# The gram's spread form with the sequence as the innermost index: one core, 32 images, windowed and axial attention

## The chip, the cores and the metric

The kernel runs on one core of one Trainium2 chip. The metric is the device time of one execution in microseconds (us), the median of several runs.

## What is computed

Two residual blocks on x of shape (32, 16, 16, 256). The first is shifted-window attention with cosine logits, a position bias, a mask and a softmax. The second, which the change is in, is axial attention without a softmax, once along the rows and once along the columns of each image. Both start with a group norm. Cut to what matters:

```python
def _self_attention(x, w_qkv, w_out, heads):          # x: sequences of 16 tokens, 256 channels
    q, k, v = jnp.split(x @ w_qkv, 3, axis=-1)         # 16 heads of 16
    dots = jnp.einsum('bhie,bhje->bhij', q, k) * d ** (-0.5)
    out = jnp.einsum('bhij,bhje->bhie', dots, v)
    return out.transpose(0, 2, 1, 3).reshape(b, t, d) @ w_out

x = x + window_attention(_gn(x), ...)                  # layer 0
h = _gn(x)                                             # layer 1
x = x + _self_attention(columns of h, w_qkv0, w_out0) + _self_attention(rows of h, w_qkv1, w_out1)
```

Since there is no softmax in the axial layer, (q kT) v is computed as q (kT v). The 16 x 16 matrix kT v of a head and a sequence is the "gram" of this kernel.

## The kernel before

Channels lie on the 128 partitions in two groups (G = 2), tokens in the free dimension. Every f16 operand of a matmul is kept as a high and a low part (value = high + low), and products are made in passes high*high, low*high, high*low. The kernel works on the images in a software pipeline written out by hand: each engine has a `step(k)` that issues, for several images at different stages, its instructions in a fixed order, with semaphore waits (`reach`) between engines. One step is one image's worth of work on every engine. The index a is 0 for the column pass and 1 for the row pass of the axial layer; everything below is done once for each a and image.

The stages that touch the gram, in order:

- `gram_matmuls` (L598 to L611, TensorE) makes kT v of 32 sequences (2 groups of 16) and 16 heads, into two PSUM banks, one for each parity of head in a pair.
- `gram_high` (L894, ScalarE) takes the two banks one after the other, scales each by a per-partition mask (a head's 16 partitions of 32) and writes the f16 high part: two ACTIVATE of 128 x 512. `gram_low` (L1347, VectorE) writes the low part, bank value times mask minus high part: two SCALAR_TENSOR_TENSOR of 128 x 512, which read the high part from SBUF. Both go through `gram_half` (L330), which says where in SBUF they write.
- `spread_gram` (L422, the queue of SyncE) copies the gram into `gram_wide`, four DMAs of 32 partitions each: `gram_wide` has four slots q of 32 columns, and partitions 32q to 32q + 31 are copied into slot q alone; the rest stays zero from a memset at the start. So each sequence has in `gram_wide` a block-diagonal 128 x 128 matrix, high and low.
- `axial_out` (L613, TensorE) multiplies: for each of 32 sequences the high matrix is loaded as the stationary operand and meets q's high and low part (32 columns, L620), then the low matrix is loaded and meets q's high part (16 columns, L621). That is 64 weight loads of 128 x 128 and 64 short matmuls for each a and image, 4,096 over the kernel.

In a step of TensorE the order is: gram_matmuls(0), axial_kv(0), window_out, a wait for `gram_lo[0]` (the low part by VectorE, as the PSUM banks are used again), gram_matmuls(1), window_v, image_channels, axial_kv(1), result_rows, axial_out(0), axial_y, scores, axial_q(1), axial_q(0), axial_out(1), window_den, window_pv, window_qk. axial_out(a) waits for `gram_spread[a]`, that is, for the landing of the four DMAs.

The per-partition layout before is, from the outermost index to the innermost: sequence s (32), [slot q (4) in gram_wide], column e (32), part t (2: high, low), of 2 bytes each.

Of the kernel before, what the change touches and what calls it, by code (L numbers as in the profile page):

```python
# [11 lines left out]
F32 = mybir.dt.float32  # L12
F16 = mybir.dt.float16

P = 128
IMAGES, SIDE, D = 32, 16, 256
TOK = SIDE * SIDE
G = D // P
HEADS, DH = 16, 16
# [4 lines left out]
SEQ = SIDE  # L24
# [36 lines left out]
def reach(eng, sem, img, per=1, j=None):  # L61

    if not missing(img.n):
        eng.wait_ge(sem, img.n * per + (per if j is None else j))


def is_first(img):
    return img.n == 0
# [39 lines left out]
def build(nc, x, Wq, Wk, Wv, bv, Wo, bo, logit_scale, cpb_w1, cpb_b1, cpb_w2, w_qkv0, w_out0, w_qkv1, w_out1,  # L108
          c_ident, c_group, c_small, c_mask, c_coords, out, scratch):
    ctx = ExitStack()  # L110
    with ctx:
        def sb(name, shape, dt=F32):
            return ctx.enter_context(nc.sbuf_tensor(name, shape, dt))

        def sem(name):
            return ctx.enter_context(nc.semaphore(name))
# [46 lines left out]
        kv32 = [sb(f"kv32_{a}", [P, 2, HALF]) for a in range(2)]  # L163
        kv = [sb(f"kv_{a}", [P, 2, 2, 2 * D], F16) for a in range(2)]
        v_wide = [sb(f"v_wide{a}", [P, 4, 2, 2, D], F16) for a in range(2)]
        gram_both = sb("gram", [P, 2, G * SEQ, 32, 2], F16)
        gram = [gram_both[:, a] for a in range(2)]
        gram_wide = [sb(f"gram_wide{a}", [P, G * SEQ, 4, 32, 2], F16) for a in range(2)]
        o1_32 = [sb(f"o1_32_{a}", [P, HALF]) for a in range(2)]
        o1 = [sb(f"o1_{a}", [P, 2, HALF], F16) for a in range(2)]  # L170
        y = sb("y", [P, HALF])
# [30 lines left out]
        wide_zeroed = sem("wide_zeroed")  # L202
# [50 lines left out]
        gram_spread = [sem(f"gram_spread{a}") for a in range(2)]  # L253
# [75 lines left out]

        def gram_half(a, head, t):  # L330

            return gram[a][:, :, DH * head:DH * head + DH, t]

        def gram_psum(a, head, img):

# [2 lines left out]
        def gram_place(g, s):  # L338

            return 16 * (s // 4 % 2) + 8 * g + 4 * (s // 8) + s % 4  # L340
# [29 lines left out]
        def _(sp):  # L370
# [51 lines left out]
            def spread_gram(a, img):  # L422

                if is_first(img):
                    sp.wait_ge(wide_zeroed, ZEROED)
                reach(sp, gram_lo[a], img)
                for q in range(4):
                    rows = slice(32 * q, 32 * q + 32)
                    sp.dma_start(gram_wide[a][rows, :, q].rearrange("p s e t -> p s (e t)"),  # L429
                                 gram[a][rows].rearrange("p s e t -> p s (e t)")).then_inc(gram_spread[a], 16)  # L430

            def spread_v_rows(a, img):

# [13 lines left out]
            def step(k):  # L447
                for img in there(k - 6):
                    spread_v_rows(0, img)
                    spread_v_rows(1, img)  # L450
                for img in there(k - 10):
                    store_image(img)
                for img in there(k - 6):
                    spread_gram(0, img)
                for img in there(k):
                    load_image(img)
                for img in there(k - 6):
                    spread_gram(1, img)
# [9 lines left out]
            spread_v_rows(1, pic[0])  # L468
            load_image(pic[4])
            spread_gram(0, pic[0])  # L470
            load_image(pic[6])
            spread_gram(1, pic[0])
# [9 lines left out]
        def _(pe):  # L482
# [130 lines left out]
            def axial_out(a, img):  # L613
                reach(pe, gram_spread[a], img, 64)
                for s in range(G * SEQ):
                    cols = slice(s * SEQ, (s + 1) * SEQ)
                    dst = ps[:, O_BANK[a](img) + s // SEQ, (s % SEQ) * 2 * SEQ:(s % SEQ + 1) * 2 * SEQ]
                    at = gram_place(*divmod(s, SEQ))
                    high, low = (gram_wide[a][:, at, :, :, gp].rearrange("p h e -> p (h e)") for gp in range(2))
                    pe.matmul(dst.rearrange("p (t i) -> p t i", t=2), high, q1[a][:, :, cols], start=True, stop=False)  # L620
                    last = pe.matmul(dst[:, 0:SEQ], low, q1[a][:, 0, cols], start=False, stop=True)  # L621
                last.then_inc(o1_done[a], 1)
# [38 lines left out]
            def step(k):  # L661
# [23 lines left out]
                for img in there(k - 4):  # L685
                    reach(pe, xt_copied, earlier(img, -4))
                    edge(pe, qk_scaled, earlier(img, -3))
                    axial_out(0, img)
# [18 lines left out]
                for img in there(k - 4):  # L707
                    reach(pe, biased[1], earlier(img, -3))
                    axial_out(1, img)
# [70 lines left out]
            pe.wait_ge(qk_scaled, 4)  # L780
            pe.wait_ge(xt_copied, 5)
            axial_out(0, pic[0])
            pe.wait_ge(gram_lo[1], 1)
            group_means(0, pic[4])
# [50 lines left out]
        def _(act):  # L835
# [58 lines left out]
            def gram_high(a, img):  # L894

                reach(act, gram_done[a], img)
                reach(act, gram_spread[a], previous(img), 64)
                for head in range(2):
                    last = act.activation(gram_half(a, head, 0), gram_psum(a, head, img), ACT.Copy,  # L899
                                          scale=gram_mask[:, head:head + 1])  # L900
                last.then_inc(gram_hi[a], 1)
# [227 lines left out]
        def _(pool):  # L1129

            pool.memset(v_diag[:].rearrange("p a b c d -> p (a b c d)"), 0.0).then_inc(zeroed, 1)
            pool.memset(gram_wide[0][:].rearrange("p s q e t -> p (s q e t)").bitcast(F32), 0.0).then_inc(wide_zeroed, 1)
            pool.wait_ge(first_in, 16 * 3)

            def zero_v_wide():
# [98 lines left out]

        @block.vector
        def _(dve):
            dve.memset(gram_wide[1][:].rearrange("p s q e t -> p (s q e t)").bitcast(F32), 0.0).then_inc(wide_zeroed, 1)
            dve.wait_ge(first_in, 16 * 3)

            def cap_scale():  # L1240
# [106 lines left out]
            def gram_low(a, img):  # L1347

                reach(dve, gram_hi[a], img)
                reach(dve, o1_done[a], previous(img))  # L1350
                for head in range(2):
                    last = dve.scalar_tensor_tensor(gram_half(a, head, 1), gram_psum(a, head, img), gram_mask[:, head:head + 1],  # L1352
                                                    gram_half(a, head, 0), ALU.mult, ALU.subtract)
                last.then_inc(gram_lo[a], 1)
# [274 lines left out]
```

## Time and profile before

| | |
|---|---|
| median of 3 runs | 912.56 us (911.0 to 913.3) |
| the profiled execution | 910.2 us, of which the span of instructions 908.4 us |
| TensorE busy | 846.0 us, 93% |
| VectorE busy | 730.3 us, 80% |
| ScalarE busy | 666.0 us, 73% |
| GpSimd busy | 493.0 us, 54% |
| mean granted TensorE clock | 0.972 of full speed |
| DMA, the queue of SyncE | 331,728 packets, 71.10 MB, 37.8% of 16 engines |

The profile is of one execution, whose own time is 1.8 us over its span. A share of busy time is a mean over start, steady steps and end. TensorE's matmuls are pipelined, so their single durations overlap; what a group of matmuls costs is read from the start of its first to the start of what follows.

### The profile page before, as it was taken

How to read it: one execution, taken by the hardware profiler on the slowest of the kernel's cores; microseconds unless marked ns; L12 is line 12 of the kernel's file. 1: busy time of each engine (PE TensorE's matmuls, PEld its weight loads, DVE VectorE, ACT ScalarE, POOL GpSimd, SP SyncE). 2: the span in 40 equal slices, each digit the busy share in tenths (PEclk: the TensorE clock that was granted, in tenths of full speed). 3: DMA queues.
4: the chain of work that ended last, by engine and by line, in shares of the span. 5: the costliest groups of instructions: out<-in, count | busy, mean ns of one | idle time of the engine just before them, and what ended most of it. 6: DMA issues, size and time to landing. Idle time of an engine off the chain costs nothing.

```text
span 908.4 us, 45985 instructions
## 1 busy us (share of the span) xinstructions
PE 846.0 (93%) x20128; PEld 660.0 (73%) x20128; DVE 730.3 (80%) x1528; ACT 666.0 (73%) x1112; POOL 493.0 (54%) x366
## 2 busy tenths in 40 slices
PE   5478899999999999999999999999999999999865
PEld 3354677777878877777877777778787777777554
DVE  7879888888888988888888888888889888886431
ACT  3666677887777787887777878877778778777441
POOL 4545455565565565565565565655655655655321
PEclk9698999999999999999999999999999999999888
DMA  6201344434334444434334444343444443343433
GB/s 165 57 13 40 74 80 80 78 77 88 78 82 82 92 91 90 84 80 90 79 78 87 86 92 91 74 88 78 85 81 91 90 92 70 72 81 78 92 74 82
DMA packets 334431, 74.04 MB, mean 82 GB/s; under 512 B 282373, under 2 KB 333719, under 8 KB 334231
## 3 DMA queue, kind: packets, MB, share of 16 engines
q1 hardware_dynamic: 331728, 71.10, 37.8%
q8 instruction: 158, 2.59, 1.3%
q10 hardware_dynamic: 2502, 0.01, 0.2%
q14 instruction: 43, 0.34, 0.1%
HBM read 12.31 MB, written 8.40 MB: 23 GB/s over the span
## 4 chain that ended last, share of the span: by engine, by line
PE 76%; SPq 7%; DVE 6%; issue 4%; DMA 3%; ACT 3%; POOL 1%; POOLq 0%; DVEq 0%; ACTq 0%
PE ps L518 20%; PE ps L588 15%; PE ps L631 9%; PE ps L620 7%; PE ps L609 6%; PE ps L535 4%; SPq L439 4%; PE ps L621 4%; PE ps L550 3%; PE ps L559 3%; PE ps L568 3%; SPq L429 2%; DMA gram_wide<-gram 2%; PE ps L658 2%; PE ps L652 1%
## 5 line engine op out<-in xcount | busy, mean ns | idle before, releaser
L1147 POOL TENSOR_TENSOR kv<-kv,kv 128x1024 f16<-128x1024 f32 x64 | 137.0, 2141 | 90.0 <-ACT kv L882 84.6
L930 ACT ACTIVATE probs<-probs 128x1024 f32<-128x1024 f32 x64 | 67.8, 1059 | 91.9 <-DVE probs L1407 89.7
L620 PEld LDWEIGHTS ps<-q,gram_wide 128*128 128x128 f16 x2048 | 107.5, 97 | 13.2 <-DMA gram_wide<-gram 5.4
L620 PE MATMUL ps<-q,gram_wide 128*128 128x32 f16 x2048 | 111.6, 177 | 5.4 <-DMA gram_wide<-gram 5.3
L1152 POOL TENSOR_TENSOR stat<-stat,small 128x2 f32<-128x2 f32 x64 | 43.3, 693 | 133.1 <-DVE stat L1326 125.3
L1352 DVE SCALAR_TENSOR_TENSOR gram<-ps,small,gram 128x512 f16<-128x512 f32 x128 | 94.5, 793 | 23.0 <-ACT gram L899 19.8
L621 PE MATMUL ps<-q,gram_wide 128*128 128x16 f16 x2048 | 110.7, 169 | 0.0
L621 PEld LDWEIGHTS ps<-q,gram_wide 128*128 128x128 f16 x2048 | 106.2, 97 | 0.4
L518 PE MATMUL ps<-xn,w_q 128*128 128x256 f16 x768 | 97.4, 278 | 7.0 <-POOL xn L1147 7.0
L899 ACT ACTIVATE gram<-ps,small 128x512 f16<-128x512 f32 x128 | 95.3, 817 | 8.0 <-PE ps L609 8.0
L1147 POOL TENSOR_TENSOR xn<-xn,xn 128x512 f16<-128x512 f32 x64 | 74.9, 1170 | 47.7 <-ACT xn L919 47.7
L631 PE MATMUL ps<-o,w_o 128*128 128x256 f16 x768 | 91.2, 276 | 3.0 <-POOL o L1147 2.8
L588 PE MATMUL ps<-w_kv,xn 128*128 128x512 f16 x384 | 90.7, 387 | 2.8 <-ACT kv L882 1.9
L588 PE MATMUL ps<-w_kv,xn_cols 128*128 128x512 f16 x384 | 90.5, 386 | 0.5 <-POOL xn_cols L1147 0.3
L1147 POOL TENSOR_TENSOR qk<-qk 128x1024 f16<-128x1024 f32 x32 | 69.0, 2157 | 38.7 <-ACT qk L950 38.7
L1147 POOL TENSOR_TENSOR o<-o,o 128x512 f16<-128x512 f32 x64 | 74.3, 1162 | 26.1 <-ACT o L913 25.8
L518 PEld LDWEIGHTS ps<-xn,w_q 128*128 128x128 f16 x768 | 71.3, 99 | 20.1 <-POOL xn L1147 5.4
L1407 DVE TENSOR_TENSOR probs<-ps,bias_mask 128x1024 f32<-128x1024 f32 x64 | 75.5, 1219 | 12.6 <-PE ps L550 12.6
L631 PEld LDWEIGHTS ps<-o,w_o 128*128 128x128 f16 x768 | 76.0, 102 | 12.6 <-POOL o L1147 3.0
L609 PE MATMUL ps<-v_wide,kv 64*32 64x128 f16 x6144 | 69.1, 225 | 11.7 <-DVE o L1358 5.6
L1147 POOL TENSOR_TENSOR xn_cols<-xn,xn_cols 128x512 f16<-128x512 f32 x32 | 45.3, 1416 | 62.4 <-ACT xn_cols L925 62.4
L1365 DVE STREAM_TRANSPOSE qk<-qk_sq 128x1024 f32<-128x1024 f32 x32 | 39.9, 1245 | 47.7 <-ACT qk_sq L935 47.7
(122 smaller groups left out, 1961.2 us busy)
## 6 DMA issues: line engine op xcount, KB each, us to landing
gram_wide<-gram SPq DMA_DIRECT2D x256, 128.0 KB, 3.1
v_wide<-kv SPq DMA_DIRECT2D x512, 32.0 KB, 2.3
x_in<-x SPq DMA_DIRECT2D x32, 128.0 KB, 2.4
x_in<-x SPq DMA_DIRECT2D x64, 64.0 KB, 2.3
out<-y_out SPq DMA_DIRECT2D x32, 128.0 KB, 2.2
out<-y_out SPq DMA_DIRECT2D x64, 64.0 KB, 2.0
x<-L_conv_w_qkv SPq DMA_DIRECT2D x1, 768.0 KB, 4.4
y_out<-L_conv_w_out SPq DMA_DIRECT2D x2, 256.0 KB, 4.8
```

Of the source, the lines that this page charges most:

```text
L518: last = pe.matmul(dst, w[:, wp, c, m * P:m * P + P], act[:, xp, c * TOK:(c + 1) * TOK], start=(n == 0), stop=(n == 5))
L588: last = pe.matmul(ps[:, KV_BANK[a](img) + t, :], xn1[a][:, xp, c * TOK + t * P:c * TOK + t * P + P], w_l1[a]["kv"][:, wp, c, :], start=(n ...
L609: last = pe.matmul(dst.rearrange("p (s e) -> p s e", e=32), kv[a][rows, kp, t, own], v_wide[a][rows, :, vp, t, own], start=(n == 0), stop= ...
L620: pe.matmul(dst.rearrange("p (t i) -> p t i", t=2), high, q1[a][:, :, cols], start=True, stop=False)
L621: last = pe.matmul(dst[:, 0:SEQ], low, q1[a][:, 0, cols], start=False, stop=True)
L631: last = pe.matmul(ps[:, Y_BANK(img), g * TOK:(g + 1) * TOK], w_l1[a]["o"][:, wp, c2, g * P:(g + 1) * P], o1[a][:, xp, c2 * TOK:(c2 + 1) * ...
L899: last = act.activation(gram_half(a, head, 0), gram_psum(a, head, img), ACT.Copy, scale=gram_mask[:, head:head + 1])
L930: act.activation(part, part, ACT.Exp).then_inc(probs_ready[g], 1)
L1147: return pool.tensor_tensor(dst, whole, high, ALU.subtract)
L1152: pool.tensor_tensor(stat[layer][:, 28:30], stat[layer][:, 26:28], minus_half, ALU.pow).then_inc(gn_pow[layer], 1)
L1352: last = dve.scalar_tensor_tensor(gram_half(a, head, 1), gram_psum(a, head, img), gram_mask[:, head:head + 1], gram_half(a, head, 0), ALU. ...
L1407: dve.tensor_tensor(probs[:, 4 * g:4 * g + 4, :].rearrange("p a n -> p (a n)"), ps[:, S_BANK[g](img):S_BANK[g](img) + 2, :].rearrange("p b ...
```

## The change

The per-partition layout of the gram and of its spread form is turned: slot q (in gram_wide), column e, sequence s, part t. So the elements of one sequence's matrix, which are the columns of a weight load, lie 128 bytes apart in place of 4 bytes; ScalarE's and VectorE's writes, and VectorE's read of the high part, walk the columns of a sequence in the same order as before and so step by 128 bytes in place of 4 too; and what one partition sends in one DMA of the spread is one run of 4,096 bytes in source and destination, in place of 32 runs of 128 bytes. The two memsets cover the same bytes. The arithmetic and its order are the same.

```diff
-        gram_both = sb("gram", [P, 2, G * SEQ, 32, 2], F16)
+        gram_both = sb("gram", [P, 2, 32, G * SEQ, 2], F16)
         gram = [gram_both[:, a] for a in range(2)]
-        gram_wide = [sb(f"gram_wide{a}", [P, G * SEQ, 4, 32, 2], F16) for a in range(2)]
+        gram_wide = [sb(f"gram_wide{a}", [P, 4, 32, G * SEQ, 2], F16) for a in range(2)]
@@ gram_half
-            return gram[a][:, :, DH * head:DH * head + DH, t]
+            return gram[a][:, DH * head:DH * head + DH, :, t].rearrange("p e s -> p s e")
@@ spread_gram
-                    sp.dma_start(gram_wide[a][rows, :, q].rearrange("p s e t -> p s (e t)"),
-                                 gram[a][rows].rearrange("p s e t -> p s (e t)")).then_inc(gram_spread[a], 16)
+                    sp.dma_start(gram_wide[a][rows, q].rearrange("p e s t -> p (e s t)"),
+                                 gram[a][rows].rearrange("p e s t -> p (e s t)")).then_inc(gram_spread[a], 16)
@@ axial_out
-                    high, low = (gram_wide[a][:, at, :, :, gp].rearrange("p h e -> p (h e)") for gp in range(2))
+                    high, low = (gram_wide[a][:, :, :, at, gp].rearrange("p h e -> p (h e)") for gp in range(2))
```

No instruction is added, removed or moved on TensorE, VectorE, ScalarE or GpSimd. On the queue of SyncE every instruction keeps its place as well; only the shape of the spread's DMAs differs. A step there before (v_wide is the spread of v, x_in a coming image, out a finished one):

```order
L439 DMA v_wide<-kv 16x4x256 x16
L429 DMA gram_wide<-gram 32x32x64 x4
L420 DMA x_in<-x 128x256
L420 DMA x_in<-x 64x256 x2
L429 DMA gram_wide<-gram 32x32x64 x4
```

and the same rows of the change:

```order
L439 DMA v_wide<-kv 16x4x256 x16
L429 DMA gram_wide<-gram 32x2048 x4
L420 DMA x_in<-x 128x256
L420 DMA x_in<-x 64x256 x2
L429 DMA gram_wide<-gram 32x2048 x4
```

Nothing moved; each of the four DMAs of a spread goes from 32 x 32 pieces of 64 elements to 32 pieces of 2,048.

## Rows read from the trace of the kernel before

**Rows 1.** The page: busy time of the engines; granted clock in 40 slices.

```profile
PE 846.0 (93%) x20128; PEld 660.0 (73%) x20128; DVE 730.3 (80%) x1528; ACT 666.0 (73%) x1112; POOL 493.0 (54%) x366
PEclk9698999999999999999999999999999999999888
```

**Rows 2.** Busy time by stretch (us from the span's start): steady state, one step, two axial_out.

```profile
core 0: us, PE busy (x) PEld busy (x) DVE busy (x) ACT busy (x) POOL busy (x), PEclk, DMA share, GB/s
200.00:800.00 600.00, 598.30 (x14647) 473.32 (x14646) 512.72 (x1105) 472.72 (x791) 344.34 (x256) 1.00 0.41 84
395.49:421.09 25.60, 25.60 (x637) 20.16 (x644) 22.08 (x47) 20.37 (x35) 14.92 (x12) 1.00 0.42 87
406.20:408.00 1.80, 1.80 (x67) 1.74 (x65) 1.80 (x4) 1.69 (x2) 1.80 (x1) 1.00 0.28 73
888.40:890.20 1.80, 1.80 (x65) 1.80 (x66) 0.00 (x0) 0.00 (x0) 0.00 (x0) 0.50 1.09 180
```

**Rows 3.** Timeline of TensorE, axial_out(0) of a steady step: start us, us, instruction.

```profile
406.27 0.18 PE L620 MATMUL ps<-q,gram_wide 128*128 128x32 f16 x1
406.30 0.17 PE L621 MATMUL ps<-q,gram_wide 128*128 128x16 f16 x1
...
407.86 0.17 PE L621 MATMUL ps<-q,gram_wide 128*128 128x16 f16 x1
```

**Rows 4.** The same view, the last axial_out of the kernel.

```profile
888.39 0.21 PE L620 MATMUL ps<-q,gram_wide 128*128 128x32 f16 x1 [3.90 <-DMA gram_wide<-gram]
...
890.10 0.17 PE L621 MATMUL ps<-q,gram_wide 128*128 128x16 f16 x1
```

**Rows 5.** The same view, gram_matmuls(1) of a steady step and what follows it.

```profile
400.47 1.00 PE L609 MATMUL ps<-v_wide,kv 64*32 64x128 f16 x96
401.40 0.39 PE L535 MATMUL ps<-w_v,xn 128*128 128x256 f16 x2
```

**Rows 6.** By source line: duration ns min/median/max, first and last start us, forms.

```profile
L919 ACT ACTIVATE xn<-xn x64: 612/630/642, 13.3 to 853.1; 128x512 f16<-128x512 f32 x64
L875 ACT ACTIVATE w_o<-y_out x2: 612/614/617, 32.6 to 46.2; 128x512 f16<-128x512 f32 x2
L875 ACT ACTIVATE w_kv<-x x1: 1045/1045/1045, 30.7 to 30.7; 128x1024 f16<-128x1024 f32 x1
L925 ACT ACTIVATE xn_cols<-xn x32: 1050/1084/1092, 58.4 to 853.6; 128x512 f16<-128x512 f32 x32
L899 ACT ACTIVATE gram<-ps,small x128: 777/819/837, 85.3 to 884.2; 128x512 f16<-128x512 f32 x128
L1352 DVE SCALAR_TENSOR_TENSOR gram<-ps,small,gram x128: 748/788/833, 87.4 to 885.7; 128x512 f16<-128x512 f32 x128
```

**Rows 7.** Timeline of ScalarE and VectorE between gram_matmuls(0) and gram_matmuls(1) of that step.

```profile
395.42 1.12 PE L609 MATMUL ps<-v_wide,kv 64*32 64x128 f16 x96
396.03 1.01 ACT L935 ACTIVATE qk_sq<-ps 128x1024 f32<-128x1024 f32 x1
396.94 1.49 ACT L899 ACTIVATE gram<-ps,small 128x512 f16<-128x512 f32 x2
398.46 1.46 DVE L1352 SCALAR_TENSOR_TENSOR gram<-ps,small,gram 128x512 f16<-128x512 f32 x2
```

**Rows 8.** Waits: who waited for whom, us in total, times, longest.

```profile
PE ps L620 <- DMA gram_wide<-gram: 5.3, 4, 3.9
```

**Rows 9.** By source line, the DMA issues of SyncE's queue: ns each.

```profile
L429 SPq DMA_DIRECT2D gram_wide<-gram x256: 585/675/2154, 88.9 to 888.6; - x128
L439 SPq DMA_DIRECT2D v_wide<-kv x512: 585/596/1828, 71.7 to 879.8; - x171
```

**Rows 10.** The page: DMA issues, KB each, median us from issue to landing.

```profile
gram_wide<-gram SPq DMA_DIRECT2D x256, 128.0 KB, 3.1
x_in<-x SPq DMA_DIRECT2D x32, 128.0 KB, 2.4
out<-y_out SPq DMA_DIRECT2D x32, 128.0 KB, 2.2
```

**Rows 11.** Groups by line and form: weight loads, busy us, mean ns | idle before.

```profile
L658 PEld LDWEIGHTS ps<-stat,group 128*128 128x128 f32 x128 | 19.4, 192 | 10.2 <-DVE stat L1312 3.4 <-ACT v_diag L964 2.2 <-issue 2.1
L620 PEld LDWEIGHTS ps<-q,gram_wide 128*128 128x128 f16 x2048 | 107.5, 97 | 13.2 <-DMA gram_wide<-gram 5.4 <-DVE probs L1407 5.3 <-issue 1.8
```

More of the change, by code:

```diff
@@ L1131, in _ @@
             pool.memset(v_diag[:].rearrange("p a b c d -> p (a b c d)"), 0.0).then_inc(zeroed, 1)
-            pool.memset(gram_wide[0][:].rearrange("p s q e t -> p (s q e t)").bitcast(F32), 0.0).then_inc(wide_zeroed, 1)
+            pool.memset(gram_wide[0][:].rearrange("p q e s t -> p (q e s t)").bitcast(F32), 0.0).then_inc(wide_zeroed, 1)
             pool.wait_ge(first_in, 16 * 3)
@@ L1236, in _ @@
         def _(dve):
-            dve.memset(gram_wide[1][:].rearrange("p s q e t -> p (s q e t)").bitcast(F32), 0.0).then_inc(wide_zeroed, 1)
+            dve.memset(gram_wide[1][:].rearrange("p q e s t -> p (q e s t)").bitcast(F32), 0.0).then_inc(wide_zeroed, 1)
             dve.wait_ge(first_in, 16 * 3)
```

## The prediction

> **What bounds the kernel now.** I read the page first: TensorE is busy 93% of the span, VectorE 80%, ScalarE 73%, GpSimd 54% [rows 1]. That is a mean over start, middle and end, so next the stretches: between 200 and 800 us TensorE is busy 598.3 of 600 us at full granted clock, and one step is 25.60 us with all of it TensorE, 22.08 VectorE, 20.37 ScalarE [rows 2]. Twenty-odd of the 32 steps look like this. In steady state TensorE is the bound and waits for nobody; what the change does to TensorE's own work arrives in full, and what it does to others arrives only past their slack.
>
> Then the stage that reads the changed buffer. axial_out issues 64 weight loads and 64 short matmuls. Its first matmul starts at 406.27 and its 64th at 407.86 [rows 3]: 1.59 us over 63 intervals is 25.2 ns for a load and its matmul. The matmuls themselves move 32 or 16 columns; at 2.4 GHz (granted clock 1.00 in that stretch, [rows 2]) that is 13 and 7 ns, so they don't set the pace. What does? Two rows speak for the weight load's read of SBUF. In the last axial_out, after a wait of 3.90 us, the granted clock is 0.50, that is 1.2 GHz [rows 2], and the pace is (890.10 - 888.39)/63 = 27.1 ns [rows 4]: half the clock, nearly the same pace, so it isn't counted in TensorE's cycles. And 96 loads with matmuls of gram_matmuls take 401.40 - 400.47 = 0.93 us, 9.7 ns each [rows 5], so the issue of instructions isn't it either. What is left is something of fixed time in loading 128 columns of f16, about 0.2 ns a column.
>
> **The change, part by part.** Nothing is added or moved; four things cost differently.
>
> (1) The weight loads, 4,096 in all. Their columns lie 128 bytes apart in place of 4. No TensorE read in the trace steps that far, so the price has to be bounded. Below: nothing, if the load doesn't care. The nearest row that shows what a wide step costs is ScalarE's. L919 and L925 are the same copy of 512 elements from f32 to f16; L925 reads them 64 bytes apart. They take 630 and 1,084 ns, 454 ns more [rows 6]. A copy of 1,024 elements takes 1,045 and one of 512 614, so an element costs 431/512 = 0.84 ns, and the wide step adds 454/512 = 0.89 ns: it costs each element about once more [rows 6]. If a weight load whose pace is a read of SBUF doubles likewise, 25.2 becomes 50.4 ns: 64 x 2 x 25.2 ns = 3.23 us a step, x 32 = 103.2 us. Above: if the load loses whatever makes it quick, the f32 load of 128 columns shows what a slow one looks like, 192 ns beside 97 [rows 11], 95 ns more, 389 us in all. I take the doubling, since it is the same memory and the same kind of step.
>
> The Trainium skill's page "SBUF — State Buffer" (under "Door 1", the note on cachelines) says that SBUF has 16-byte lines and that at least two accesses must fall in a line for full speed. A step of 4 bytes has four f16 in a line, one of 128 bytes has one. ScalarE's pair of rows agrees; no row shows it for TensorE. By that rule the load is slowed, the sum of this step is of the kind taken above, and the rule speaks against this change.
>
> (2) ScalarE's and VectorE's halves of the gram, 128 instructions each, two and two for each a. They write with a step of 128 bytes in place of 4, and VectorE also reads the high part so. Per stream and instruction: at least nothing (the rows show no wide write), at most L925's 0.454 us. A step of theirs that matters is a = 0: gram_matmuls(0) starts at 395.42, ScalarE squares first (396.03 for 1.01), then its two (396.94 for 1.49), VectorE's two (398.46 for 1.46, so to 399.92), and gram_matmuls(1), which waits for them, starts at 400.47 [rows 5, 7]. Slack 0.55 us. Queued behind ScalarE's pair are the high part of o1 and the copies of kv; behind VectorE's the sum over heads, whose users come later; behind the wait on TensorE all of the step. With (1) slower, TensorE comes to this place 1.6 us later in each step and the square is no longer late: its pair can start some 0.35 us sooner after gram_matmuls(0), slack 0.9 us. The six streams (two instructions on ScalarE with one, two on VectorE with two) cost 0 to 2.72 us; I take half, 1.36, as nothing shows a write: 0.46 us late, x 32 = 15 us. Both ends: 0 and (2.72 - 0.9) x 32 = 58 us. For a = 1 there is more room: axial_out(1) comes near the end of the step.
>
> (3) The spread's DMAs: 32 pieces of 4,096 bytes each in place of 1,024 of 128. Landing takes 3.1 us; loads and stores of the same 128 KB in longer runs take 2.4 and 2.2 [rows 10]. Issue takes 675 ns, for v_wide 596 [rows 9]. So up to 0.9 us + 4 x 0.08 = 1.2 us a spread, but TensorE waited for a spread four times in the whole kernel, 5.3 us, 3.9 of it once, at the end [rows 8]. In steady state this transfer is hidden behind TensorE's other work, and halving it buys nothing. I take 3 us (0 to 5).
>
> [...] TensorE's steady step has no wait in it and its matmuls go at the pace of their columns, so I book 0.
>
> Sum against the profiled execution's own 910.2 us (span 908.4): + 103.2 + 15 - 3 = 1,025.4. The median of the runs shown is 912.56, 2.4 above it: 1,027.8, so 1,028.
>
> **The rivals.**
>
> *The load doesn't care, and the writers do.* The 25.2 ns may be a floor under any full-array pair, with the load's own time well below it, so that even a doubled load stays hidden. Against it stands that the pace hardly moved with the clock, which a floor of fixed time would explain too. Then only (2) is left, with slack 0.55: (1.36 - 0.55) x 32 = 26 us, less 3: 936 us; bounds 912 and 979. VectorE would also come close to being the bound itself: 22.08 + 4 x 0.91 = 25.7 of 25.6 us a step.
>
> The Trainium skill's "TensorE: Matmul & The Clock Gate", "Back-to-back issue gap", gives matmuls of 1 to 64 columns a floor of about 60 cycles, some 25 ns, and its section on fast weight load names packed or strided columns as its read pattern, with steps far over 64 elements allowed. By these rules the load could be free in this change. The trace agrees on 25 ns at 2.4 GHz; at 1.2 GHz it shows 27.1 [rows 4], where 60 cycles would be 50.
>
> *Nothing shows.* Neither load nor writers care, or their surcharge stays in the slack, and the DMA's gain is a microsecond or two: 911 us.
>
> *The other side: faster.* All of that, and the spread lands about a microsecond sooner wherever the chain passes through it. It is decided by the fill and the drain: three or four spreads of the first and last images at 1.2 us each, bounded by the 5.3 us of waits [rows 8]. 912.6 - 4 = 908.6 us. It needs the surcharge on the load to be under about 0.3 ns (1.2 us over 4,096), and the writers' under the slack.
>
> *The load falls to the slow form.* 25.2 becomes some 120 ns, + 389 us: 1,300 us. Nothing in the trace speaks for it but that a step so wide is new.
>
> **How the numbers follow.** Chances: doubled load 0.50; load unchanged with late writers 0.15; nothing shows 0.11; faster 0.18; slow form 0.06. What can be told from no change is about 0.3%, 2.7 us. Slower is the first, the second and the last: 0.71; same 0.11; faster 0.18. The doubled load's own range is 990 (a surcharge of three quarters of the load) to 1,071 (912.6 + 103 + 58 - 3). The range for all must reach down to the cases that leave the load alone: 908 to 1,071, which leaves out the slow form, half of the faster case and the fringe of the first, some 0.17.
>
> **What the profile after would show.** Step 1: the pace of axial_out, first start to 64th, near 3.2 us in place of 1.59; the step 25.6 to about 29 us; VectorE's and ScalarE's share falling as the span grows. If the pace is unchanged, step 1 is wrong, and with it the forecast. Step 2: L899 and L1352 above 819 and 788 ns, and a wait of TensorE at gram_matmuls for VectorE's gram; if their means stand, the 15 us are wrong. Step 3: some 8,000 packets in place of 262,144 for the spread, DMA share far below 37.8%, landing under 3.1 us, and no gain from it in the middle of the kernel. The wait before the last axial_out under 3.9 us.

## The result, and the profile after

The changed kernel takes 1,500.26 us (median of 4 runs, 1,499.76 to 1,502.17) against 912.93 us of the kernel before: a ratio of 1.644, 95% interval 1.639 to 1.648. The forecast's direction was right and its size was far off: 587 us more, where 115 were forecast and 158 were the top of the range.

The page of the changed kernel, to be held against [rows 1] and the packets in the table of before:

```profile
PE 1243.7 (83%) x20128; PEld 996.5 (66%) x20128; DVE 992.1 (66%) x1528; ACT 879.9 (59%) x1112; POOL 498.0 (33%) x366
...
PEclk8886878788887878787878788878888787878766
...
q1 hardware_dynamic: 77776, 71.10, 19.6%
...
gram_wide<-gram SPq DMA_DIRECT2D x256, 128.0 KB, 2.7
```

Every engine but GpSimd is busy for longer, TensorE no longer all the time, and the granted clock, which was full through the whole middle [rows 1, 2], lies at 0.7 or 0.8 in 37 of 40 slices. The DMAs did what was asked: a quarter of the packets, half the share, landing in 2.7 in place of 3.1 us [rows 10].

Then the lines that the change touches, by source line (duration ns min/median/max), to be held against [rows 6]:

```profile
L620 PEld LDWEIGHTS ps<-q,gram_wide x2048: 162/217/254, 107.8 to 1485.2; 128*128 128x128 f16 x187
...
L899 ACT ACTIVATE gram<-ps,small x128: 2534/2682/2828, 88.3 to 1466.7; 128x512 f16<-128x512 f32 x128
...
L1352 DVE SCALAR_TENSOR_TENSOR gram<-ps,small,gram x128: 2500/2690/2995, 93.2 to 1471.9; 128x512 f16<-128x512 f32 x128
```

ScalarE's and VectorE's instructions on the gram went from 819 and 788 ns to 2,682 and 2,690, both by 1.9 us. The same part of a steady step as in [rows 3, 5, 7] (timeline: start us, us, instruction, the idle time before it and its releaser):

```profile
713.20 1.00 PE L609 MATMUL ps<-v_wide,kv 64*32 64x128 f16 x96
...
714.25 4.85 ACT L899 ACTIVATE gram<-ps,small 128x512 f16<-128x512 f32 x2
716.73 1.47 PE L518 MATMUL ps<-o,w_o 128*128 128x256 f16 x12
719.13 4.78 DVE L1352 SCALAR_TENSOR_TENSOR gram<-ps,small,gram 128x512 f16<-128x512 f32 x2 [3.53 <-ACT gram L899]
723.97 1.48 PE L609 MATMUL ps<-v_wide,kv 64*32 64x128 f16 x96 [5.77 <-DVE gram L1352]
...
731.66 0.26 PE L620 MATMUL ps<-q,gram_wide 128*128 128x32 f16 x1 [0.50 <-ACT x_t L989]
...
734.46 0.23 PE L621 MATMUL ps<-q,gram_wide 128*128 128x16 f16 x1
...
737.27 0.23 PE L621 MATMUL ps<-q,gram_wide 128*128 128x16 f16 x1
```

Between 713.20 and 723.97 the reader sees the chain of [rows 7] stretched: ScalarE's pair 4.85 us in place of 1.49, VectorE's pair 4.78 in place of 1.46, and TensorE idle for 5.77 us before gram_matmuls(1). From 731.66 to 737.27 the 64 loads of axial_out go at 5.61/63 = 89 ns, where they went at 25.2. And busy time by stretch, to be held against [rows 2]: one step, its axial_out(0), and axial_y behind it.

```profile
core 0: us, PE busy (x) PEld busy (x) DVE busy (x) ACT busy (x) POOL busy (x), PEclk, DMA share, GB/s
713.20:757.60 44.40, 38.13 (x630) 30.82 (x629) 30.33 (x47) 27.00 (x34) 14.98 (x12) 0.81 0.20 49
731.66:737.36 5.70, 5.70 (x65) 5.70 (x65) 5.63 (x7) 2.76 (x3) 2.21 (x1) 0.70 0.02 4
737.80:741.80 4.00, 4.00 (x25) 3.02 (x26) 3.97 (x9) 2.33 (x6) 0.00 (x0) 0.63 0.18 40
```

A step is 44.40 us in place of 25.60. In axial_out TensorE is shown busy without a gap and its granted clock still falls; it comes out of it at 1.2 GHz and runs the next stage so.

From the starts of TensorE's stages in this step and in that of before, the 18.80 us come out in full:

| where in the step | before, us | after, us | more |
|---|---|---|---|
| axial_out(0) and (1), start to next start | 1.67 + 1.69 | 5.70 + 5.76 | 8.10 |
| window_out to gram_matmuls(1), the wait for the gram | 1.40 | 7.24 | 5.84 |
| result_rows to axial_out(0), a wait for ScalarE | 0.52 | 1.10 | 0.58 |
| axial_y (L631) | 2.62 | 4.06 | 1.44 |
| window_den and window_pv (L559, L568) | 1.98 | 3.22 | 1.24 |
| gram_matmuls(1) and window_v (L609, L535) | 2.26 | 3.56 | 1.30 |
| all else | 13.46 | 13.76 | 0.30 |

The last four rows, 4.3 us, are for the most part stages whose own work didn't change and that stand behind a slow axial_out or behind the wait, at the lower clock.

### The profile page after: what moved, and what is told of

Read it like the earlier page. It is cut to its first block, busy times and chain, and to the rows that moved or that the text cites. A ratio compares the mean times of both kernels' runs of the same rounds, so it can differ in the third digit from the quotient of the medians.

```text
span 1498.6 us, 45985 instructions
## 1 busy us (share of the span) xinstructions
PE 1243.7 (83%) x20128; PEld 996.5 (66%) x20128; DVE 992.1 (66%) x1528; ACT 879.9 (59%) x1112; POOL 498.0 (33%) x366
## 4 chain that ended last, share of the span: by engine, by line
PE 58%; issue 16%; ACT 15%; DVE 10%; DMA 0%; SPq 0%; POOL 0%; ACTq 0%; POOLq 0%; DVEq 0%
PE ps L620 13%; PE ps L518 12%; ACT gram L899 11%; PE ps L621 10%; PE ps L631 9%; DVE gram L1352 6%; PE ps L559 4%; PE ps L568 3%; PE ps L609 2%; PE ps L550 2%; DVE head_sum L1372 2%; PE ps L658 1%; PE ps L588 1%; ACT head_rnorm L942 1%; ACT x_t L988 1%
## 5 line engine op out<-in xcount | busy, mean ns | idle before, releaser
L1352 DVE SCALAR_TENSOR_TENSOR gram<-ps,small,gram 128x512 f16<-128x512 f32 x128 | 316.9, 2683 | 141.8 <-ACT gram L899 141.8
L620 PEld LDWEIGHTS ps<-q,gram_wide 128*128 128x128 f16 x2048 | 361.6, 216 | 32.9 <-ACT x_t L989 20.2
L620 PE MATMUL ps<-q,gram_wide 128*128 128x32 f16 x2048 | 367.2, 244 | 18.6 <-ACT x_t L989 13.5
L621 PE MATMUL ps<-q,gram_wide 128*128 128x16 f16 x2048 | 365.4, 233 | 0.0
L621 PEld LDWEIGHTS ps<-q,gram_wide 128*128 128x128 f16 x2048 | 363.4, 217 | 0.0
L899 ACT ACTIVATE gram<-ps,small 128x512 f16<-128x512 f32 x128 | 311.1, 2685 | 17.3 <-PE ps L609 17.0
L609 PE MATMUL ps<-v_wide,kv 64*32 64x128 f16 x6144 | 80.8, 268 | 186.4 <-DVE gram L1352 182.0
L609 PEld LDWEIGHTS ps<-v_wide,kv 64*32 64x32 f16 x6144 | 67.5, 105 | 202.4 <-DVE gram L1352 190.9
L631 PE MATMUL ps<-o,w_o 128*128 128x256 f16 x768 | 137.2, 361 | 2.4 <-POOL o L1147 2.4
L631 PEld LDWEIGHTS ps<-o,w_o 128*128 128x128 f16 x768 | 102.3, 136 | 34.7 <-POOL o L1147 2.8
L892 ACT ACTIVATE q<-ps 128x512 f16<-128x512 f32 x64 | 37.9, 592 | 113.4 <-PE ps L621 107.6
L907 ACT ACTIVATE o<-ps 128x512 f32<-128x512 f32 x64 | 38.1, 595 | 107.3 <-PE ps L621 107.3
```

The costliest lines, as they stand in the source:

```text
L609: last = pe.matmul(dst.rearrange("p (s e) -> p s e", e=32), kv[a][rows, kp, t, own], v_wide[a][rows, :, vp, t, own], start=(n == 0), stop= ...
L631: last = pe.matmul(ps[:, Y_BANK(img), g * TOK:(g + 1) * TOK], w_l1[a]["o"][:, wp, c2, g * P:(g + 1) * P], o1[a][:, xp, c2 * TOK:(c2 + 1) * ...
```

## The experiments

**Four theories at the start.** A: three prices add up, slow loads, slow writers, and a clock that falls behind the slow loads as well as behind the wait. B: the clock falls only where TensorE waits. C: loads and writers slow each other at the memory. D: VectorE's busy time alone is the bound. Where columns land permuted the values differ and the work does not. "One run" below means a time without an interval. The kernel before lay between 908.6 and 915.4 us in all of its runs beside these, and every such time is at least 239 us away from it, but for that of side_f32_wide (916.64), which can't be told from no change; there the duration of one instruction is what is read.

**loads_wide: only the loads are wide.**

```diff
 (the changed kernel, with the gram and the writers of before)
-        gram_both = sb("gram", [P, 2, 32, G * SEQ, 2], F16)
+        gram_both = sb("gram", [P, 2, G * SEQ, 32, 2], F16)
-            return gram[a][:, DH * head:DH * head + DH, :, t].rearrange("p e s -> p s e")
+            return gram[a][:, :, DH * head:DH * head + DH, t]
```

> Only the weight loads step by 128 bytes; ScalarE, VectorE and the gram buffer are as before, and the spread moves the same 4,096-byte runs (the gram's columns land permuted, so the values are not the reference's; no work is left out). Theory A (three prices that add up: slow loads, slow writers, and a clock that falls behind the slow loads as well as behind the wait): the pace of axial_out is 89 ns as in the changed kernel, 8.2 us more a step, and the clock still falls after each of the two axial_out, about 2.9 us more a step: 36.7 us a step, about 1,260 us; the writers stay at 0.82 and 0.79 us. Rival B (the clock falls only because TensorE waits for the gram): full clock, 33.8 us a step, about 1,175 us. Rival C (loads are slow because slow writers hold the memory): pace 25 ns, about 913 us.

Measured: 1,276.24 us, ratio 1.398 (1.390 to 1.406). One step of it, its axial_out(0), axial_y, window_den with window_pv, in the columns of [rows 2]:

```profile
724.94:762.46 37.52, 37.52 (x630) 30.68 (x629) 22.55 (x47) 20.68 (x34) 15.04 (x12) 0.82 0.25 59
735.73:741.30 5.57, 5.57 (x67) 5.57 (x65) 3.20 (x9) 1.75 (x2) 1.95 (x1) 0.84 0.45 101
741.30:746.50 5.20, 5.20 (x28) 3.83 (x28) 1.25 (x5) 2.59 (x6) 0.00 (x0) 0.52 0.18 43
755.95:759.50 3.55, 3.55 (x82) 2.48 (x80) 1.55 (x4) 2.56 (x4) 0.74 (x1) 0.50 0.36 100
```

TensorE has no idle time in the step, and the clock is at 0.52 and 0.50 behind both axial_out: B falls. The pace is 5.57 us for 64 loads with the writers fast, so C falls for the loads. Of 11.92 us more a step, 7.85 are the loads themselves and 4 the clock behind them. A held, 16 us over its number.

**turned_walk: the changed kernel, with the writers' loops the other way round.**

```diff
 (the changed kernel; [...] stands for the two banks)
-            return gram[a][:, DH * head:DH * head + DH, :, t].rearrange("p e s -> p s e")
+            return gram[a][:, DH * head:DH * head + DH, :, t]
-            return ps[...].rearrange("p b (x e) -> p (b x) e", e=32)[:, :, DH * head:DH * head + DH]
+            return ps[...].rearrange("p b (x e) -> p (b x) e", e=32)[:, :, DH * head:DH * head + DH].rearrange("p s e -> p e s")
```

> The changed kernel with ScalarE's and VectorE's walk turned: sequences innermost, so writes and the read of the high part step by 4 bytes again, and PSUM is read with a step of 128 bytes instead. Layout, spread and weight loads stay those of the change. Theory A (the writers pay for the step of consecutive writes to SBUF): L899 and L1352 fall to between 0.8 and 1.3 us, the wait for the gram is at most 1 us a step, and the time is that of loads_wide, about 1,260 us. Rival E (it is the layout as a whole, or any operand with a wide step, PSUM's too): they stay at 2.7 us, about 1,500 us.

Measured: 1,276.01 us, ratio 1.398 (1.389 to 1.406). The writers by source line:

```profile
L899 ACT ACTIVATE gram<-ps,small x128: 805/831/845, 86.3 to 1242.8; 128x512 f16<-128x512 f32 x128
...
L1352 DVE SCALAR_TENSOR_TENSOR gram<-ps,small,gram x128: 773/794/948, 88.4 to 1244.3; 128x512 f16<-128x512 f32 x128
```

The same layout, the same bytes; only the order in which an instruction writes them changed, and 2.68 and 2.69 us became 0.83 and 0.79, while PSUM is now read in steps of 128 bytes, which costs ScalarE 12 ns. E falls: the price is of the step between consecutive accesses to SBUF (high_wide, below, tells the write from the read). It gives back 224 us of the 587.

**writers_wide: only the writers are wide.**

```diff
 (the kernel before)
-        gram_both = sb("gram", [P, 2, G * SEQ, 32, 2], F16)
+        gram_both = sb("gram", [P, 2, 32, G * SEQ, 2], F16)
-            return gram[a][:, :, DH * head:DH * head + DH, t]
+            return gram[a][:, DH * head:DH * head + DH, :, t].rearrange("p e s -> p s e")
-                                 gram[a][rows].rearrange("p s e t -> p s (e t)")).then_inc(gram_spread[a], 16)
+                                 gram[a][rows].rearrange("p e s t -> p (e s t)").rearrange("p (x y) -> p x y", y=64)).then_inc(gram_spread[a], 16)
```

> Only ScalarE's and VectorE's halves of the gram step by 128 bytes; gram_wide, the weight loads with 4-byte steps and the 128-byte runs of the spread are as before (the columns land permuted; no work is left out). Theory A: the writers take 2.7 us each as in the changed kernel, TensorE waits some 6 us a step at gram_matmuls(1) and runs some 1.3 us a step at the low clock behind it: 33 us a step, about 1,150 us; pace of axial_out 25 ns. Rival C (loads and writers slow each other): the writers stay near 0.8 us and the time near 913 us. Rival D (VectorE's busy time alone is the bound, 22.1 + 4 x 1.9 = 29.7 us a step): about 1,045 us.

Measured: 1,363.26 us, ratio 1.493 (1.484 to 1.502). All of the numbers were too low; the writers take 2.69 and 2.61 us as A said (so C falls for the writers too), but the step is 39.3 us, not 33. A step by busy time:

```profile
616.03:655.33 39.30, 30.21 (x632) 22.40 (x630) 30.01 (x47) 26.86 (x35) 14.87 (x12) 0.87 0.27 54
```

The gram's pieces in the chain of waits of the next step (start us, us, what):

```profile
658.66 2.79 ACT gram L899
...
663.61 2.65 DVE gram L1352
...
668.52 2.81 ACT gram L899 x2
...
677.02 4.79 DVE gram L1352 x2
```

TensorE is busy 30.21 of 39.30 us and VectorE 30.01: no engine is the bound, a chain is. It goes round the step through both passes' pairs: gram_high(0), gram_low(0), the sum over heads that is queued behind it on VectorE, its square roots on ScalarE, gram_high(1) queued behind these, the image copy queued behind that, the image's statistics on VectorE, gram_low(1), and from there the mask of k, the biases and the softmax's sums to the next step. Each of the four pairs grew by some 3.35 us, 13.4 us in all; by the two spans a step is (1,362.4 - 908.4)/32 = 14.2 us longer. That 25.60 + 13.4 = 39.0 comes so near to the 39.3 of this step is in part luck: 25.60 was TensorE's work, and how long this chain was before was not measured. D falls too.

**rows_wide: the writers of one pass only.**

```diff
 (the kernel before)
+            if a == 1:
+                turned = gram[a].rearrange("p s e t -> p (s e) t").rearrange("p (e s) t -> p e s t", s=G * SEQ)
+                return turned[:, DH * head:DH * head + DH, :, t].rearrange("p e s -> p s e")
             return gram[a][:, :, DH * head:DH * head + DH, t]
```

> The kernel before with the writers of the row pass alone (a = 1) in steps of 128 bytes; the column pass, the spread and the loads as before (columns of one pass permuted; no work left out). The prediction held that a = 1 has room. Theory S (all four pairs of the gram lie one after the other in one chain round the step, 25.6 + 4 x 3.35 = 39.0 us for writers_wide): with two pairs slow 25.6 + 6.7 less a little slack, 31 to 32 us a step, 1,090 to 1,120 us. Theory of the prediction: 913 to 930 us.

Measured: 1,152.43 us, one run. A step of it:

```profile
562.63:596.57 33.94, 28.40 (x629) 21.66 (x628) 27.24 (x48) 23.57 (x34) 14.80 (x11) 0.90 0.31 63
```

33.9 us in this step, 8.3 more, and 7.6 by the two spans, (1,150.6 - 908.4)/32, where two slow pairs are 6.7: S is the right kind and was put too low. Where the rest comes from stays open. It is not shown to be the clock (mean 0.90): the granted clock is below full from 568.0 to 580.3 us alone (0.84, then 0.64), where the chain runs through ScalarE and VectorE, and 1.00 where it comes back to TensorE. The pass that the prediction gave room costs more than half of writers_wide's surcharge (239 of 449 us).

**high_wide: a wide write, and a wide read beside a narrow write.**

```diff
 (the kernel before)
+            if t == 0:
+                turned = gram[a].rearrange("p s e t -> p (s e) t").rearrange("p (e s) t -> p e s t", s=G * SEQ)
+                return turned[:, DH * head:DH * head + DH, :, 0].rearrange("p e s -> p s e")
             return gram[a][:, :, DH * head:DH * head + DH, t]
```

> The kernel before with the high part alone written in steps of 128 bytes by ScalarE; VectorE reads it so but writes the low part in steps of 4 bytes; spread and loads as before (columns permuted; no work left out). Theory A (it is the write that costs, a wide read about one element time more): L899 2.7 us, L1352 0.79 + 0.45 = 1.2 us, and TensorE's wait for the gram about half of that of writers_wide: 3.8 + 0.9 - 0.55 = 4.1 us a step, about 1,060 us. Rival F (a wide read costs as much as a wide write): L1352 2.7 us and the time of writers_wide, about 1,150 us.

Measured: 1,194.61 us, one run; its lines are shifted by three.

```profile
L902 ACT ACTIVATE gram<-ps,small x128: 2534/2682/2836, 86.2 to 1166.6; 128x512 f16<-128x512 f32 x128
...
L1355 DVE SCALAR_TENSOR_TENSOR gram<-ps,small,gram x128: 1076/1094/1158, 91.1 to 1170.5; 128x512 f16<-128x512 f32 x128
```

VectorE pays 306 ns for reading 512 elements in wide steps, 0.6 ns each, and ScalarE 1,863 ns for writing as many, 3.6 ns each. F falls. The whole was 135 us above A's number. The chain through both passes' pairs accounts for it: four writes at 1.863 us and four reads at 0.306 us more are 8.7 us a step, and by the two spans it is (1,192.8 - 908.4)/32 = 8.9.

**step8, step16, step32, step64: where does the price begin?** The layout with K sequences inside the column (K = 2, 4, 8, 16; 1 is the kernel before, 32 the change). VectorE's instruction is cut in 2, 4, 4 and 2 pieces, as it takes only two free dimensions.

```diff
 (the kernel before; KS = 2, 4, 8 or 16; the writers' and the spread's lines, turned to match, are left out)
-        gram_both = sb("gram", [P, 2, G * SEQ, 32, 2], F16)
+        gram_both = sb("gram", [P, 2, G * SEQ // KS, 32, KS, 2], F16)
-        gram_wide = [sb(f"gram_wide{a}", [P, G * SEQ, 4, 32, 2], F16) for a in range(2)]
+        gram_wide = [sb(f"gram_wide{a}", [P, G * SEQ // KS, 4, 32, KS, 2], F16) for a in range(2)]
-                    high, low = (gram_wide[a][:, at, :, :, gp].rearrange("p h e -> p (h e)") for gp in range(2))
+                    high, low = (gram_wide[a][:, at // KS, :, :, at % KS, gp].rearrange("p h e -> p (h e)") for gp in range(2))
```

> The layout halfway: two sequences inside the column, so a column's step is 8 bytes for writers and loads and a run of the spread 256 bytes; VectorE's instruction is cut in two (256 elements each) since it takes only two free dimensions. Everything is computed. Theory L (the price starts where fewer than two accesses fall in 16 bytes): nothing costs more, pace of axial_out 25 ns, L899 0.82 us; VectorE's extra starts cost 0.6 us a step inside its slack: 913 us within 0.5%. Theory G (the price grows with every doubling of the step): pace above 27 ns, 920 to 950 us.

> Four sequences inside the column: step 16 bytes, runs of 512 bytes, VectorE's instruction in four. Everything is computed. Theory L: every access is a new line from here on, so the loads are at the changed kernel's 89 ns and the writers at 2.7 us already: about 1,500 us. Theory G: loads 35 to 50 ns, L899 about 1.1 to 1.3 us: 1,000 to 1,100 us.

> Eight sequences inside the column: step 32 bytes, runs of 1,024 bytes, VectorE's instruction in four. Everything is computed. Theory L: as the changed kernel, pace 89 ns and L899 2.7 us, about 1,500 us. Theory G: loads 50 to 70 ns, L899 1.5 to 2 us, 1,150 to 1,300 us.

> Sixteen sequences inside the column: step 64 bytes, runs of 2,048 bytes, VectorE's instruction in two. Everything is computed. Theory L: pace 89 ns, L899 2.7 us, about 1,500 us. Theory G: loads 65 to 80 ns, L899 2 to 2.4 us, 1,300 to 1,400 us.

Measured, with the kernel before, the change and pad144 (below) beside them; the pace of a load is (start of the 64th - start of the first)/63 of an axial_out in the middle of the run (within a run they differ by up to 4.5 ns):

| step of a column | load, ns | ScalarE's write of 512 (median ns) | whole kernel, us |
|---|---|---|---|
| 4 bytes (before) | 25.2 | 819 | 913 |
| 8 (step8) | 33.2 | 1,406 | 1,058.8, ratio 1.162 (1.156 to 1.169) |
| 16 (step16) | 60 | 2,664 | 1,421.0, ratio 1.557 (1.549 to 1.565) |
| 32 (step32) | 62 | 2,550 | 1,405.6, one run |
| 64 (step64) | 62.5 | 2,626 | 1,424.4, one run |
| 128 (the change) | 89 | 2,682 | 1,500.3 |
| 144 in gram_wide alone (pad144) | 61 | 830 | 1,159.7, one run |

ScalarE's line in step8 and step16:

```profile
L900 ACT ACTIVATE gram<-ps,small x128: 1375/1406/1423, 85.4 to 1028.1; 128x512 f16<-128x512 f32 x128
```

```profile
L900 ACT ACTIVATE gram<-ps,small x128: 2522/2664/2809, 86.6 to 1392.7; 128x512 f16<-128x512 f32 x128
```

The writers: 512 elements touch 128, 256 and 512 pieces of 16 bytes at steps of 4, 8 and 16 bytes, and from there on 512. ScalarE's time goes with that count: 587 ns for the second 128, 1,258 for the next 256, that is 4.6 and 4.9 ns for each, and flat behind it. The Trainium skill's "SBUF — State Buffer" (under "Door 1") names lines of 16 bytes, and the place of the knee agrees; that two accesses to a line are enough for full speed does not, neither for the load (33.2 ns) nor for the write (1,406 ns). Neither theory held as a whole. L was right on the writers' plateau, but wrong on step8 and on the loads' plateau (60 to 62.5 ns, not 89); G was right that step8 pays, but too low there (920 to 950 us, where 1,059 were measured), and wrong on the writers from 16 bytes on. The loads have the same knee, and then one more rise, at 128 bytes. Of step8's 146 us the loads are 33 (8.0 ns, 4,096 times); the rest was not taken apart further.

**pad144: is the last rise the distance or the step of 128?**

```diff
 (turned_walk)
-        gram_wide = [sb(f"gram_wide{a}", [P, 4, 32, G * SEQ, 2], F16) for a in range(2)]
+        gram_wide = [sb(f"gram_wide{a}", [P, 4, 32, G * SEQ + 4, 2], F16) for a in range(2)]
-                    sp.dma_start(gram_wide[a][rows, q].rearrange("p e s t -> p (e s t)"),
-                                 gram[a][rows].rearrange("p e s t -> p (e s t)")).then_inc(gram_spread[a], 16)
+                    sp.dma_start(gram_wide[a][rows, q, :, 0:G * SEQ].rearrange("p e s t -> p e (s t)"),
+                                 gram[a][rows].rearrange("p e s t -> p e (s t)")).then_inc(gram_spread[a], 16)
```

> turned_walk with a column's step in gram_wide padded from 128 to 144 bytes; runs of the spread are 128 bytes again. Everything is computed. The pace of axial_out was 60 to 62 ns at steps of 16, 32 and 64 bytes and 88 at 128. Theory P (the last rise is a conflict of a step of 128 bytes): pace 60 to 63 ns, 1,276 - 4,096 x 0.026 = 1,170 us or less. Rival (it is the distance): pace 88 ns or more, about 1,280 us.

Measured: 1,159.72 us, one run. First and last matmul of an axial_out:

```profile
585.87 0.24 PE L620 MATMUL ps<-q,gram_wide 128*128 128x32 f16 x1
...
589.72 0.21 PE L621 MATMUL ps<-q,gram_wide 128*128 128x16 f16 x1
```

3.85/63 = 61 ns: theory P. The last rise is not the distance; it belongs to a step of 128 bytes, and with 144 bytes 116 us come back, although the runs of the spread are 128 bytes again.

**parts_apart: the other way, a step of 2 bytes.**

```diff
 (the kernel before)
-        gram_both = sb("gram", [P, 2, G * SEQ, 32, 2], F16)
+        gram_both = sb("gram", [P, 2, 2, G * SEQ, 32], F16)
-        gram_wide = [sb(f"gram_wide{a}", [P, G * SEQ, 4, 32, 2], F16) for a in range(2)]
+        gram_wide = [sb(f"gram_wide{a}", [P, 2, G * SEQ, 4, 32], F16) for a in range(2)]
 (the lines that write, spread and load it, turned to match, are left out)
```

> High and low part in separate halves of the gram and of its spread form: a column's step is 2 bytes, a run of the spread 64 bytes (524,288 in all). Everything is computed. Theory L2 (a write costs 4.9 ns for each 16-byte line that it fills only in part, else 0.84 ns an element; a load has a floor of 25 ns that is not the lines): L899 falls from 819 to about 650 ns, L1352 from 788 to about 680, pace of axial_out stays at 25.2 ns, and as TensorE is the bound the time stays at 913 us within 0.5%. Theory M (the loads too are paid by the line at every step): pace 17 to 21 ns, 890 to 900 us. Either way the shorter runs can make the spread late, 10 to 30 us.

Measured: 1,019.6 us, ratio 1.118 (1.114 to 1.122). ScalarE's writer by source line:

```profile
L899 ACT ACTIVATE gram<-ps,small x128: 667/684/707, 86.4 to 994.5; 128x512 f16<-128x512 f32 x128
```

The spread in the same kernel: how long its issue holds SyncE's queue (ns min/median/max), its landing, and the engines' shares of the chain that ended last (SPq is SyncE's queue, issuing):

```profile
L429 SPq DMA_DIRECT2D gram_wide<-gram x256: 591/1007/3015, 89.9 to 1002.4; - x128
gram_wide<-gram SPq DMA_DIRECT2D x256, 128.0 KB, 4.4
SPq 61%; PE 13%; issue 8%; DVE 8%; DMA 6%; ACT 3%; POOL 1%; POOLq 0%; DVEq 0%; ACTq 0%
```

And TensorE's wait for it (us in total, times, longest):

```profile
PE ps L620 <- DMA gram_wide<-gram: 86.1, 42, 6.3
```

The writers fell to 684 and 743 ns, where 650 and 680 were forecast, and the pace stayed at 25.1 to 25.4 ns: L2 held for both in kind, so before the change ScalarE paid some 135 ns for its step of 4 bytes, and the load stood on a floor. Those 135 ns are for going from 64 to 128 pieces of 16 bytes, 2.1 ns for each, less than half of what the further ones cost.

The time was not the 913 us of L2. A spread in runs of 64 bytes costs twice: it lands in 4.4 us in place of 3.1 [rows 10], and each issue holds the queue for 1,007 ns in place of 675 [rows 9]. The queue of SyncE is now in the way: 61% of the last chain are its issues, where 7% were before, and it waits for VectorE's gram 13.7 us in all, where it waited 79.7. TensorE waits for the spread 42 times, 86 us, where it waited 4 times, 5.3 us [rows 8]; I had put that at 10 to 30 us. These waits are 81 of the 107 us. The rest was not taken apart; the mean granted clock is 0.937 in place of 0.972, and axial_y's matmuls (L631) are busy 118.7 us in place of 91.2.

**side_f32_wide: is it the line filled in part, or the two bytes?**

```diff
 (the kernel before, ScalarE's copy at L907)
-                act.activation(along(o1_32[a][:], 1), by_token(ps[...], 1, a),
+                act.activation(along(o1_32[a][:], 0), by_token(ps[...], 1, a),
```

> The kernel before, with ScalarE's copy of the output's second half (L907, 512 elements of f32) writing in steps of 64 bytes (columns land permuted; no work left out). It tells whether a line written in part costs the same whatever the type. Theory L2: 512 lines, L907 goes from 597 to about 2,650 ns. Rival (the price is one of 2-byte elements): below 1,100 ns.

Measured: 916.64 us, one run.

```profile
L907 ACT ACTIVATE o<-ps x64: 1019/1055/1071, 100.1 to 901.0; 128x512 f32<-128x512 f32 x64
```

Writes of 4 bytes in steps of 64 take 1,055 ns where they took 597 in a row, 0.9 ns an element more, as wide reads do [rows 6]; writes of 2 bytes in steps of 64 take 2,626 (step64). L2 falls in this part: a line filled in part is not enough for the high price. At the same step the two rows differ in the size of the element, 4 bytes and 2; turned_walk, with the same buffer and the same mask as the f16 write, took 831 ns, so these are not the reason.

## Why the prediction was wrong

**What bounds the kernel.** Right: TensorE had no slack, and the pace of axial_out is not counted in its cycles. The latter held in the changed kernel too: from 734.46 to 737.27, at a granted clock of 0.50, 32 loads take 2.81 us, 88 ns each; in loads_wide, from 735.73 to 738.49 at 1.00, they take 2.76 us, 86 ns. What the prediction concluded from it, that the 25.2 ns were the load's read of SBUF, is not borne out: parts_apart halved the columns' step and the pace stayed. At steps of 8 and 16 bytes (33.2 and 60 ns for 64 and 128 pieces of 16 bytes) a piece costs 0.42 ns; by that the 32 pieces of a step of 4 bytes would take some 20 ns, an estimate, hidden under a floor of 25.2. What makes the floor stays open.

**Step (1), "I take the doubling".** Right that the load pays, wrong in size: 25.2 to 89 ns is 3.5 times, 8.10 us a step or 259 us in all, where 103 were booked. The row that priced it, a ScalarE read in steps of 64 bytes, showed one element time more; TensorE at the same step shows 62.5 ns, 2.5 times, and the change's 128 bytes add a rise of their own (62 to 89 ns, gone at 144), which no row of before could show. The upper bound, the slow load, was above it, but the range was not drawn to there.

**Step (2), "at most L925's 0.454 us".** This is the step that failed most, together with the next: a wait of 0.46 us a step was booked, and 6.42 were measured. A read stood in for a write, and a price for elements of 4 bytes for one of 2. high_wide and side_f32_wide show both halves of the error: a wide read costs VectorE 0.31 us per instruction and a wide f32 write ScalarE 0.46 us, about what was booked; a wide f16 write costs 1.86. The bound from above was no bound.

**Step (2), "For a = 1 there is more room".** Wrong, and shown by rows_wide. I read the slack of one wait of TensorE. What mattered were the two in-order queues behind the gram's instructions: with each pair 3.35 us longer, the pairs of both passes, on both engines, lie in one chain round the step. In the changed kernel the slower axial_out takes over part of the round (TensorE is 58% of the last chain there, 19% in writers_wide), and 6.4 us a step of waits are left (5.84 + 0.58), 205 us, where 15 were booked.

**The clock: not in the sum at all.** 4.3 us a step, 138 us. All of the prediction's durations were at full clock, since the steady part of before had no other [rows 2]. loads_wide shows that the loads alone bring it down, with TensorE shown busy for the whole step; the rows of axial_y and window_den at 0.50 to 0.52 are what it costs. In step8, whose loads go at 33.2 ns, the granted clock of an axial_out is 1.00 (536.3 to 538.4).

**Step (3).** Right: packets, share, issue (591 ns) and landing (2.7 us) fell, and nothing came of it, as the transfer was hidden. TensorE's waits for a spread are 3.8 us in all, where they were 5.3 [rows 8], and the wait before the last axial_out is 0.68, where it was 3.90; the one before it waits 3.11.

**Step (4), booked at 0.** No run shows a gain or a loss from fewer packets on the engines' own accesses: ScalarE's copy at L907, which the change doesn't touch, took 597 ns before and 597 after.

So 8.1 + 6.4 + 4.3 = 18.8 us a step, 602 us over 32 steps, against 590 us measured between the two spans (1,498.6 - 908.4); the fill and the drain have fewer full steps. The three parts are not those of the experiments one by one, since loads_wide (+ 362 us) and writers_wide (+ 449 us) overlap to 587: each hides part of the other's waits.

**The rivals.** "The load doesn't care" falls: the load goes at 89 ns. Its first half, a floor with the load's own time below it, is what parts_apart points to, but a load that costs 60 ns and more does not stay under it. The Trainium skill's "TensorE: Matmul & The Clock Gate" ("Back-to-back issue gap") gives a floor of about 25 ns for so few columns; the 25.2 ns at steps of 2 and 4 bytes agree, and a wide step goes far over it. "Nothing shows" and "faster" fall with the load. The slow form (some 120 ns, 1,300 us) was not met either: 89 ns, and its 389 us held nothing of the waits and the clock, which make the larger part of the 587. The range's error is one of method: I let the cases that leave the load alone pull it down to 908, and gave the case above the doubling 0.06.

None of the versions tried is faster than the kernel before; its 4-byte step with runs of 128 bytes lies between two losses, the writers' and loads' at a step of 8 bytes and the spread's at runs of 64.

## What to carry to other kernels

Before lengthening a DMA's runs by turning a layout, look at what the compute engines' steps become: here a hidden transfer was improved and 4,096 weight loads and 256 writes paid for it. Shortening the runs has its own price, on the queue that issues them as well as on the landing (parts_apart). If the layout must stay, turn the loop of the writers so that consecutive writes stay within 16 bytes (turned_walk, 224 us), and avoid a column step of exactly 128 bytes for weights (pad144, 116 us more, one run). A price taken from a read does not bound a write, nor one of f32 a price of f16; and the slack of one wait does not bound an instruction that grows, when two in-order queues carry it round the step.

## What the runs showed of the hardware

- A f16 write of ScalarE costs 4.6 to 4.9 ns for every further 16-byte piece that it touches, from 128 pieces on (819, 1,406, 2,664 ns for 128, 256, 512 pieces), and 2.1 from 64 to 128 (684 to 819). VectorE's instruction pays 1,902 ns from 128 to 512 pieces, of which high_wide's wide read is 306, which leaves some 4.2 ns a piece for the write, an estimate. An f32 write in steps of 64 bytes costs only 0.9 ns an element more. Why the 2-byte write is so dear stays open.
- A 128-column f16 weight load goes at 25 ns for steps of 2 and 4 bytes, 33 at 8, 60 to 62.5 at 16 to 64 and at 144, 89 at 128. Why 128 stands out stays open; no other multiple of 128 bytes was tried.
- The granted clock fell inside axial_out with TensorE shown busy 5.70 of 5.70 us, when its loads took 89 ns each; at a pace of 25.2 ns (before) and of 33.2 (step8) it was full.
- A DMA of 128 KB in a spread from SBUF to SBUF landed in 4.4, 3.1 and 2.7 us with runs of 64, 128 and 4,096 bytes, and one of 64-byte runs held the queue for 1,007 ns where 128-byte runs took 675.
- PSUM read in steps of 128 bytes cost ScalarE 12 ns in 819 and VectorE 6 in 788 (turned_walk).
